# The hand-over from a tokenizer to a selective scan: bank pairs, folds and bias work placed anew, and routing weights in four operations

## The reference

```python
# 1: attention of a pooled query over the 16 pixels of its 4 x 4 patch, 8 heads
reduce_feats = x.mean((3, 5))                      # 256 tokens for each image
q = _ln(reduce_feats) @ Wq.T;  k, v = _ln(unf) @ Wkv.T
h = reduce_feats + softmax(q k) v @ proj_w.T + proj_b
# 2: a selective scan along the 256 tokens of an image
x_proj, Bm, C, delta = (_layernorm(h) @ W + b for each)
A_bar = exp(-softplus(delta));  u = (1 - A_bar) * Bm * x_proj
h = h + (C * scan(A_bar, u)) @ Wy + by
# 3: a binary tree of 255 nodes, 8 levels; each token walks down by the sign of its score
score = x . w1s[current] + b1s[current]            # 8 scores on the path
out = sum over levels of (x @ w2s[node] + b2s[node]) * gelu(|score|)
```

## Time and profile before

| what | value |
|---|---|
| median of 3 runs | 729.01 us (727.99 to 730.46) |
| the profiled execution | 729.95 us, its span 728.1 us |
| PE busy | 633.0 us (87%) |
| DVE busy | 555.6 us (76%) |
| ACT busy | 461.6 us (63%) |
| POOL busy | 465.7 us (64%) |

### The profile page before, as it was taken

One profiled execution on the slowest core, in us unless ns is written; L12 is line 12 of the kernel. 1 busy time (PEld: TensorE's weight loads), 2 busy tenths in 40 slices (PEclk: granted clock), 3 DMA queues, 4 the chain that ended last, 5 costly groups with the idle time before them and its releaser, 6 DMA issues.

```text
span 728.1 us, 16646 instructions
## 1 busy us (share of the span) xinstructions
PE 633.0 (87%) x5290; PEld 328.6 (45%) x5290; DVE 555.6 (76%) x1053; ACT 461.6 (63%) x931; POOL 465.7 (64%) x448
## 2 busy tenths in 40 slices
PE   1599999999999999996799889885169999999995
PEld 1122222222222222222456555543068788788884
DVE  1278888898988888898469768788367777777873
ACT  0587777777777777751588768674046656665663
POOL 5846888798888888555604545567705556655656
PEclk9999999999999999997899999999569999999998
DMA  8033333333333221000079720001122222222110
GB/s 322 32 117 117 116 116 117 116 116 118 117 116 117 110 101 40 2 12 1 5 130 158 177 93 34 30 29 45 49 62 54 55 54 55 52 50 54 49 36 2
DMA packets 49070, 57.80 MB, mean 79 GB/s; under 512 B 31970, under 2 KB 44788, under 8 KB 46890
## 3 DMA queue, kind: packets, MB, share of 16 engines
q1 hardware_dynamic: 43882, 50.11, 23.2%
q0 software_dynamic: 5120, 6.84, 2.9%
HBM read 50.03 MB, written 10.28 MB: 83 GB/s over the span
## 4 chain that ended last, share of the span: by engine, by line
PE 37%; issue 4%; DVE 3%; POOL 3%; another core or an unknown queue 1%; ACT 1%; DMA 1%; SPq 0%; DVEq 0%; ACTq 0%; POOLq 0%
PE mixed_bank L1877 12%; PE turned0a L1859 3%; PE turned1a L1859 3%; POOL rows_by_group L1153 2%; PE s_proj L1562 2%; PE back_bank L1884 2%; PE s_logits L1656 2%; PE turned0b L1864 1%; PE turned1b L1864 1%; PE s_delta L1584 1%; PE s_proj L1597 1%; PE s_proj L1572 1%; PE s_proj L1596 1%; PE s_ln L1641 1%
## 5 line engine op out<-in xcount | busy, mean ns | idle before, releaser
L1897 POOL DMA_INDIRECT out<-orow,m_rows x96 | 107.4, 1119 | 91.7 <-ACT orow L1842 67.2
L812 PE MATMUL s_proj<-x_px,w_kv 64*64 64x512 f32 x256 | 133.6, 606 | 0.0
L809 PE MATMUL s_proj<-x_px,w_kv 64*64 64x512 f32 x256 | 133.5, 606 | 0.0
L1791 DVE TENSOR_TENSOR m_xs<-m_rows 128x768 f32<-128x768 f32 x96 | 91.3, 952 | 26.7 <-ACT m_rows L1823 21.3
L496 POOL TENSOR_TENSOR pre<-va 128x1024 f32<-128x1024 f32 x32 | 76.2, 2381 | 40.2 <-DVE va L593 40.2
L1153 POOL DMA_INDIRECT rows_by_group<-r_pay,r_slot_i x64 | 69.7, 1089 | 44.8 <-DVE r_slot_i L1476 27.1
L475 POOL TENSOR_TENSOR half_px<-x_px 128x1024 f32<-128x1024 f32 x32 | 75.8, 2369 | 35.1 <-DMA x_px<-in_x 29.3
L1877 PE MATMUL mixed_bank<-m_xsT,m_w_cur 128*64 128x128 f32 x1344 | 88.9, 276 | 4.7 <-issue 4.5
L579 DVE TENSOR_TENSOR qk<-s_proj,q 128x512 f32<-128x512 f32 x128 | 86.6, 679 | 7.6 <-PE s_proj L812 6.3
L593 DVE TENSOR_TENSOR va<-b_a,v_sb 128x512 f32<-128x512 f32 x128 | 84.9, 685 | 8.0 <-PE b_a L827 7.9
L1877 PEld LDWEIGHTS mixed_bank<-m_xsT,m_w_cur 128*64 128x64 f32 x1344 | 73.9, 137 | 15.1 <-issue 14.8
(11 more groups left out here) (274 smaller groups left out, 1685.7 us busy)
## 6 DMA issues: line engine op xcount, KB each, us to landing
x_px<-in_x SPq DMA_DIRECT2D x16, 2048.0 KB, 8.0
m_rows<-rows_by_group SPq DMA_DIRECT2D x96, 72.0 KB
wt<-in_w2T SPq DMA_DIRECT2D x8, 512.0 KB
rows_by_group<-rows_by_group SPq DMA_DIRECT2D x1, 2286.0 KB
out<-orow,m_rows POOLq DMA_INDIRECT x96
rows_by_group<-r_pay,r_slot_i POOLq DMA_INDIRECT x64
wt<-in_w2T SPq DMA_DIRECT2D x2, 256.0 KB
wt<-in_w2T SPq DMA_DIRECT2D x4, 128.0 KB
```

Of the source, the lines that this page charges most:

```text
L809: mm(b_k[i][LO, :], w_kv[LO, 0, LO], px(t, j, LO), start=True, stop=True)
L812: mm(b_k[i][HI, :], w_kv[HI, 0, HI], px(t, j, HI), start=True, stop=True).then_inc(done["kv_product"], 1)
L1791: d.tensor_tensor(xs[:, i % RING, :, :], rows[:, i, X0:X0 + C].rearrange("p (o c) -> p o c", o=1).broadcast_to([P, UNITS, C]), rows[:, i, ...
L1897: nc.gpsimd.indirect_dma_start(out_d, bass.IndirectOffsetOnAxis(ap=rows[:, i, ID0:ID0 + 1].bitcast(I32), axis=0), orow[:, i, :], None, bou ...
```

## The change

- **Bank pairs.** In the last tile, spreads 1 and 3 go to the pair of banks that keys used (`b_k`), spreads 0 and 2 to `b_a`. Spread i then waits for the products of spread i - 2 only. `inputs_first` uses those banks and waits for all of the last tile's products.
- **Folds.** The second half of the last tile is folded by VectorE (`fold_end`: an add of 1024 elements, an add of 512, a reduction of 1024 to 256) in place of GpSimd's four operations. The first half stays on GpSimd.
- **Bias parts** move from VectorE to GpSimd, ahead of tile 13's folds. Zeroing moves there too, ahead of tile 12's folds, with the part masks and the identity matrix, which was made behind the barrier. The load of b1 has a semaphore of its own and goes first.
- **Second image.** `inputs_second` (eight matmuls) and five ScalarE operations on the second image's decay run ahead of the barrier; behind it project_bx(0, 1) and those five are left out, project_y comes first with a bank of its own, and VectorE starts with gate(0, 1).
- **Path weights.** Four operations on pairs of columns in place of eight on single ones, with the intermediates in unused columns of the rows. The token number is an operation ahead of them. For the last chunk the four run on VectorE.

Its core (semaphore counts and unchanged guards cut). The loop over t with `zero_front` and the loop over c are GpSimd's; `zero_front` there waits for the slot of tile 13 and then, ahead of its last memsets, for that of tile 14. `path_weights` there ends with chunk 6, `scatter` waits for weights and token numbers, and `last_weights` is VectorE's:

```diff
+    def spread_to(t, i):
+        return b_k if t == TILES - 1 and i % 2 else b_a
...
-            if m > 0:
+            if t == TILES - 1 and i > 0:
+                pe.wait_ge(done["va_ready"], m - 2)
+                pe.wait_ge(done["qk_ready"], NCH * TILES)
+            elif m > 0:
                 pe.wait_ge(done["va_ready"], m)
...
+        def fold_end():
+            v.wait_ge(done["va_ready"], NCH * t + 8)
+            v.wait_ge(done["quartered"], 2 * t + 1)
+            d.tensor_tensor(p1, va2[:, :, 0:2, :], va2[:, :, 2:4, :], ALU.add)
+            d.tensor_tensor(dst, p1[:, :, :, 0, :], p1[:, :, :, 1, :], ALU.add)
+            d.tensor_reduce(pre4[:, :], pre2[:, :, :].rearrange("p h (w u) -> p (h w) u", u=S), AX.X, ALU.add)
...
         for t in range(TILES + 4):
+            if t == TILES:
+                zero_front()
+                part_masks()
             if t == TILES + 1:
-                part_masks()
+                bias_parts()
...
+        def inputs_second():
+            pe.wait_ge(f["is_gated_y"], 1)
+            for at, kind in ((0, 1), (TOK, 0)):
+                for b in range(2):
+                    j = mm(b_p2[:, b, at:at + TOK], f["w_p"][half(b), kind, :], f["xn2"][half(b), 1, :], start=True, stop=True)
...
+    def weight_steps(q):
+        return ((right, mags, on(5)), (left, mags, right), (last[:, :, :, 1], both, on(6)), (last[:, :, :, 0], both, last[:, :, :, 1]))
...
         for c in range(CHN):
+            token_ids(c)
             path_weights(c)
             scatter(c)
...
+            if t - 3 == CHN - 1:
+                last_weights()
...
-        spread2(1, 0)
         project_y(0, 0)
+        spread2(1, 0)
+        centre3(0, 0)
         project_d(1, 0)
-        project_bx(0, 1)
-        centre3(0, 0)
```

More of the change, by code:

```diff
@@ L964, in _ @@
             spread(t - 2, 2)
+            if t == TILES + 1:
+                delta_first(0)
+        inputs_second()
 I32 = mybir.dt.int32
@@ L1000, in scan_and_route @@
     pw = sb("pw", [P, 2, QC, 2])
-    right, left = (sb(n, [P, QC]) for n in ("right", "left"))
     grp = sb("grp", [P, QC])
@@ L1112, in _, with token_ids @@
         for q in range(2):
-            g.memset(pay[:, q, :, ID0 + 1:ROW], 0.0)
-        m = [0]
-        def done(ins):
-            ins.then_inc(weights, 1)
-            m[0] += 1
-            return ins
+            g.memset(pay[:, q, :, ID0 + 3:ROW], 0.0)
+        def token_ids(c):
+            if not live(c):
+                return
+            if c > 1:
+                pool.wait_ge(scattered[c % 2], 16 * QC * (c // 2))
+            g.iota(pay[:, c % 2, :, ID0:ID0 + 1].bitcast(I32), pattern=[[P, QC], [0, 1]], base=P * QC * c, channel_multiplier=1).then_inc(ids, 1)
         def path_weights(c):
-            if not live(c):
+            if not 0 <= c < CHN - 1:
                 return
@@ L1161, in _, with decayed_early @@
         a = nc.scalar
+        def decayed_early(c, k):
+            return 2 * c + k < 2
         def square2(c, k):
@@ L1476, in slots, with last_weights @@
             d.tensor_copy(slot_i[:, q, :], slot[:, :]).then_inc(slots_ready, 1)
+        gate(0, 1)
         normalise2(1, 0)
-        gate(0, 1)
+        def last_weights():
+            c = CHN - 1
+            q = c % 2
+            v.wait_ge(magnitudes, 2 * c + 2)
+            v.wait_ge(weights, 4 * c)
+            v.wait_ge(scattered[q], 16 * QC * (c // 2))
+            (r0, a0, b0), (r1, a1, b1), (r2, a2, b2), (r3, a3, b3) = weight_steps(q)
+            d.tensor_tensor(r0, a0, b0, ALU.mult).then_inc(weights, 1)
+            v.wait_ge(weights, 4 * c + 1)
+            d.tensor_tensor(r1, a1, b1, ALU.subtract).then_inc(weights, 1)
+            v.wait_ge(weights, 4 * c + 2)
+            d.tensor_tensor(r2, a2, b2, ALU.mult).then_inc(weights, 1)
+            v.wait_ge(weights, 4 * c + 3)
+            d.tensor_tensor(r3, a3, b3, ALU.subtract).then_inc(weights, 1)
         for t in range(2, CHN + 3):
```

209 lines of the change are left out of this document (115 added, 94 removed).

## The result

| kernel | median | ratio to before, 95% interval |
|---|---|---|
| before | 728.72 us (20 runs) | |
| changed | 724.30 us (20 runs) | 0.994 (0.9917 to 0.9962), -4.4 us |

The forecast was 723.4, in a range from 720.2 to 727.8. The changed kernel's profiled execution took 727.52, with a span of 725.8, so it is 3.2 above its own median.

The account below looks back on a forecast made before the run. TensorE was taken as full in the tokenizer's steady part, with the gain at two seams, the last tile's drain and the routing's end. -3.5 - 0.4 - 1.75 = -5.65 gave a median of 723.4 us, range 720.2 to 727.8.

Parts of the forecast that it names:

- The drain, -3.5: End of the tokenizer: last engine arrives at the barrier at 351.0 instead of 354.50, -3.5 us (bounds 0 and -4).
- the 3.2 forecast: Last tile's fold on VectorE: `fold_end` takes 3.2 us with waits and is done at 345.6.
- the arrival of the last engine: Before the barrier: ScalarE ends last at 351.0, after a delta product of 1.0 us and five decay operations.
- Behind the barrier, -0.4: From barrier to VectorE's first use of the second image's output: low clock at first, returning inside, -0.4 us (bounds +1, -2.7).
- the rival's 2.7: Rival: TensorE's clock is high behind the barrier, the distance becomes 8, -2.7 us there, span 721.1; chance 0.17.
- The end, -1.75: End of routing: chunk 7's weights on VectorE, first scatter at 515.7 instead of 517.48, -1.75 us (bounds -1.5, -2.2).
- that rival: End of routing: VectorE's four weight operations hold up chunk 6's scatters, at worst 1.0 us, time 724.4; chance 0.07.
- for chunks 0 to 6: nothing: Routing: the new path weights gain nothing in chunks 0 to 6, since GpSimd waits for slots there anyway.
- The head start lost in the routing: Rival: routing waits do not move with the barrier, so only the end's gain is left, 727.3; chance 0.10.
- GpSimd's cover: Tokenizer: 1.3 us cover hides bias parts of 5.6; rival: beyond 6.9 they delay VectorE's product one for one; chance 0.11.
- The term of 0.25 for GpSimd's new work: Tokenizer: zeroing ahead of tile 12's folds delays VectorE's product of 309.76; 0.25 us charged (bounds 0 and 0.85).
- The low level through the whole drain: Rival: TensorE's clock stays low in the drain, last product at 344.6, only -0.4 and -1.75 remain, 726.9; chance 0.12.

Follow-up runs that it names:

- e9: Changed kernel with the last tile's four spreads back on one pair of banks, bias parts still on GpSimd; 0.995 against before.
- e6: Changed kernel, unchanged, run and profiled again in the third session; 0.9916 against before, -5.9 us.
- e5: Kernel before, unchanged, profiled again in the third session; span 695.8 us, median of before there 700.1 us.
- e10: Changed kernel with tile 15's second half folded on GpSimd again instead of by VectorE's `fold_end`; 0.9921 against before.
- e1: Kernel before with only the change's path weights, chunk 7's on VectorE and token numbers made ahead; 0.9968 against before, -2.2 us.
- e3: Changed kernel with seven more ScalarE operations ahead of the barrier as a delay; 1.0014 against before.
- e7: Changed kernel without the ten bias-part operations on GpSimd, their sum set to zero, so the first bias is left out; 0.9904 against before.
- e2: Changed kernel with the old path weights put back, leaving the drain and the start behind the barrier; 0.996 against before, -2.8 us.
- e4: Changed kernel with SP's loads of the mixing's tables held back until chunk 2's slots are ready; 0.9931 against before.
- e8: Changed kernel with GpSimd's zeroing and masks one step later and the last six bias-part operations behind the barrier; 0.9887 against before, -7.9 us.
- e11: Changed kernel with two unused 512-column matmuls filling TensorE's wait for the last fold; 0.9893 against before, -7.8 us.

## Why the prediction was right, and where it was not

The forecast of -5.65 us stands against -4.4 (-6.1 to -2.8) in the first session and -5.9 (-7.6 to -4.3) in the third. The sum holds, but its terms changed places, and that it came so near is in part luck. By the marks and an estimate from them, the changed kernel gains about 4 us when the level behind the barrier is low (1.5 at the barrier, 0 behind it, 2.5 from the weights) and about 7.4 when it is high (2.1, 2.8 and 2.5); -5.65 lies between the two.

**The drain, -3.5.** The last product was forecast for 342.3 and came at 341.6 to 342.0. The step behind it named two causes, bias parts and banks. By e9's marks the banks carry 4.4 and bias parts 0.8. The reading of the earlier trace rows that the cast "holds the queue" was right for 1.5 us at the third spread, of which half is gone again at the last product. `fold_end` took the 3.2 forecast, but began 0.67 late, as GpSimd's half had to be there first. The step that failed is the arrival of the last engine: 351.0 forecast, 352.45 found (351.82 + 0.63). It assumed delta at the high level, 1.0, and the level had fallen at 347.05, 0.5 us behind TensorE's idle 2.44: 1.91 and ScalarE's start at 349.02, not 347.6. That is 0.9 of the 1.45, and the later fold 0.5. In e6 it is another engine that comes last, TensorE at 353.1 with `inputs_second` at the low level, which the forecast had done by 350.6. The barrier gained 2.1 (1.5 from e5 to e6), not 3.5. The scans fell from 2.44 to 1.27, as the earlier trace rows let expect, and off the path; in e10, where GpSimd folds beside them again, the two take 2.27.

**Behind the barrier, -0.4.** At the low level the distance to chunk 0's slots is 36.7 to 36.8 in before, e1, e3, e6 and e7 alike: the distance gains 0, not 0.4. The low level lasts longer there in the changed kernel, though (8.6 us behind the barrier in e6, 6.6 in before), so a small gain of the reordering may be hidden in it. At the high level the distance is 33.9, so 2.8 less, a tenth off the rival's 2.7. Both cases happen to one and the same kernel. The rival was no other mechanism but the other outcome of a toss, and its chance of 0.17 was too low: the changed kernel's hand-over has the high level in three of four profiles (changed, e2, e4; not e6).

**The end, -1.75.** The gap fell from 2.50 to 0.99 in the first session, 2.44 to 0.99 in the others: -1.5, the lower bound, because GpSimd needs 0.81 from the token numbers to the scatter and not the 0.59 assumed. VectorE's four operations are hidden, and the scatters stand 1.27 apart as before, so that rival falls. But "for chunks 0 to 6: nothing" was wrong: -1.0 comes from there (e1 against e5), since VectorE's comparisons are shorter with the new weights, by a cause that is open.

**The head start lost in the routing.** The first trace after looked just like this rival: 4.9 us ahead at chunk 0, 1.3 behind at chunk 7. e2, e3 and e6 refute it. A delay of 7.3 arrives as 7.2, and 3.6 of head start as 3.6. The unexplained waits of the earlier trace rows are there in both kernels, in some sessions and not in others.

**GpSimd's cover.** The mildest form came true. Bias parts took 7.2 instead of 5.6, 0.3 beyond the 6.9 at which the prediction put the end of the cover, and the product of 326.56 came at 326.76 though the tokenizer ran 0.37 ahead. The term of 0.25 for GpSimd's new work was too small: counted from a product of VectorE 70.6 us ahead of it in before, the last tile's `weigh` comes 0.6 to 0.7 late in e2, e3, e4, e6 and e9 (0.9 in the first profile of changed), 0.4 in e7, which has the zeroing alone, and not at all in e8. So the zeroing costs 0.4 and bias parts 0.2. The low level through the whole drain did not occur in any profile of the changed kernel; e10 had it for most of the spreads, with the last product at 344.2 where the rival said 344.6.

## What to carry to other kernels

Where two engines hand a pair of buffers back and forth, look at who idles once the blocking work is gone: moving work off one of them gained 0.8 us here and lost nearly all of it again, mostly through the engine that took the work over; the second pair gained 4.4. A short wait of TensorE can cost twice, once by itself and once by the level of the work behind it, so price a step at both levels. Whether it pays to fill such a wait is not settled here: shortening it (e8) did as well as filling it (e11). One profile after a change shows one execution: read the stage marks of several, before a loss between two of them gets a story.

## What the runs showed of the hardware

- The distance from the barrier to the first slots takes two values, 33.9 to 34.0 and 36.7 to 37.0 us, by the level of TensorE's clock, with 35.4 once where it returned at 358.
- On GpSimd a bfloat16 multiplication of 128x256 by one value for each partition takes 0.92 us, more than twice a cast of the same size (0.39 to 0.40), and more than a two-input addition (0.67).
- Sessions, or the chips they ran on, differ by up to 30 us for the same kernel (699.0 and 700.1 against 728.7 and 729.0). In the routing the difference goes with waits that have no releaser in the profile, and the mixing is 17 us longer too (194.8 against 177.5).
